# Linear attention and its tail: one elementwise step and one mask more taken off VectorE, the order changed, the expert layer begun inside the tail, and a weight test moved under the experts

## The reference, cut to what matters

```python
q = (elu(q) + 1.0) * scale
k = elu(k) + 1.0
attn = einsum('bhld,bhmd->bhlm', qi, ki) * causal
num = einsum('bhlm,bhme->bhle', attn, vi) + einsum('bhld,bhde->bhle', qi, S)
den = attn.sum(-1) + einsum('bhld,bhd->bhl', qi, Z)
out = num / maximum(den, 1e-06)
```

## Time and profile before

| | |
|---|---|
| median of 3 runs | 1272.51 us |
| the profiled execution: time, span | 1273.35 us, 1271.5 us |
| busy: TensorE, VectorE, ScalarE, GpSimd | 1152.8, 986.7, 771.9, 568.4 us |
| start to the first q and k | 0 to 26 us |
| linear attention, sequences 0 to 15 | 26 to 207 us |
| its tail | 207 to 237 us |
| experts | 237 to 436 us |
| softmax attention and FFN | from 437 us on |

### The profile page before, as it was taken

One profiled execution on the slowest core, in us unless ns is written; L12 is line 12 of the kernel. 1 busy time (PEld: TensorE's weight loads), 2 busy tenths in 40 slices (PEclk: granted clock), 3 DMA queues, 4 the chain that ended last, 5 costly groups with the idle time before them and its releaser, 6 DMA issues.

```text
span 1271.5 us, 32080 instructions
## 1 busy us (share of the span) xinstructions
PE 1152.8 (91%) x10554; PEld 941.7 (74%) x10554; DVE 986.7 (78%) x2499; ACT 771.9 (61%) x2314; POOL 568.4 (45%) x729
## 2 busy tenths in 40 slices
PE   3888886789898869999999999999999997999997
PEld 3555554688888747777777777777777766999997
DVE  6688885588888777778788778787877876788885
ACT  2445553222222249888989888899888894344342
POOL 2777775444444554444545445445444342011112
PEclk9999998799999989999999999999999998999999
DMA  8000000000000000000000000000000000000000
GB/s 282 10 2 0 0 1 2 1 2 1 0 1 0 1 1 2 1 2 1 2 2 1 0 0 0 0 0 0 0 0 0 2 1 1 6 13 12 8 12 19
DMA packets 14303, 12.32 MB, mean 10 GB/s; under 512 B 1778, under 2 KB 12564, under 8 KB 13972
## 3 DMA queue, kind: packets, MB, share of 16 engines
q1 hardware_dynamic: 14228, 11.34, 2.9%
HBM read 9.24 MB, written 2.10 MB: 9 GB/s over the span
## 4 chain that ended last, share of the span: by engine, by line
PE 56%; DVE 14%; issue 8%; POOL 4%; ACT 1%; DVEq 1%; POOLq 0%; ACTq 0%
PE bank L191 14%; PE bank L976 10%; PE bank L1041 10%; PE bank L1070 10%; PE bank L1083 5%; PE bank L840 4%; POOL rstd L365 2%; DVE stat L298 2%; DVE hT L1230 1%; DVE gg L1222 1%; PE bank L795 1%; DVE yn L314 1%; POOL X L370 1%; DVE mv L303 1%; DVE fh_hi L1191 1%
## 5 line engine op out<-in xcount | busy, mean ns | idle before, releaser
L993 ACT ACTIVATE work<-bank,work 128x256 f32<-128x256 f32 x512 | 236.0, 474 | 60.0 <-DVE work L985 59.2
L985 DVE TENSOR_REDUCE work<-bank 128x2 f32<-128x512 f32 x256 | 164.0, 682 | 113.2 <-PE bank L976 113.2
L1007 POOL TENSOR_TENSOR work<-work 128x512 f32<-128x512 f32 x64 | 66.7, 1041 | 279.0 <-DVE work L1001 279.0
L959 POOL TENSOR_TENSOR work<-work 128x512 f32<-128x512 f32 x128 | 164.3, 1284 | 30.2 <-DVE work L951 15.8
L1013 ACT ACTIVATE work<-work 128x256 f32<-128x256 f32 x384 | 161.7, 509 | 0.0
L1041 PE MATMUL bank<-ident,work 128*128 128x128 f32 x1024 | 141.9, 279 | 5.1 <-DVE work L949 1.6
L1041 PEld LDWEIGHTS bank<-ident,work 128*128 128x128 f32 x1024 | 111.7, 141 | 38.5 <-issue 19.9
L1070 PE MATMUL bank<-work 128*64 128x256 f32 x1024 | 138.5, 392 | 0.5 <-DVE work L1056 0.5
L840 PE MATMUL bank<-WrT,moe_work 128*128 128x128 f32 x1024 | 137.4, 278 | 0.7 <-POOL moe_work L817 0.7
L363 POOL TENSOR_SCALAR ve<-mv 128x2 f32<-128x2 f32 x128 | 28.6, 223 | 240.1 <-DVE mv L303 240.1
L976 PE MATMUL bank<-work 32*128 32x256 f32 x2048 | 130.4, 391 | 2.6 <-ACT work L993 1.6
(11 more groups left out here) (176 smaller groups left out, 2903.9 us busy)
## 6 DMA issues: line engine op xcount, KB each, us to landing
X<-in_x SPq DMA_DIRECT2D x4, 512.0 KB, 5.9
wF<-in_L_ffn_h_w SPq DMA_DIRECT2D x2, 1024.0 KB, 9.7
out<-X SPq DMA_DIRECT2D x16, 128.0 KB, 1.8
w_qkv<-in_L_attn_w_qkv SPq DMA_DIRECT2D x1, 1536.0 KB, 9.2
WrT<-in_L_ffn_Wr SPq DMA_DIRECT2D x1, 1024.0 KB, 5.1
w_out<-in_L_attn_w_out SPq DMA_DIRECT2D x1, 512.0 KB, 10.5
wF<-in_L_ffn_w_w SPq DMA_DIRECT2D x2, 256.0 KB, 8.5
rope_sin<-in_rope_sin SPq DMA_DIRECT2D x1, 256.0 KB, 3.2
```

Of the source, the lines that this page charges most:

```text
L959: nc.gpsimd.tensor_tensor((QT if kind == "q" else KT)[:, p, a, :], rc[:, ru % 2, :], rs_[:, ru % 2, :], ALU.add).then_inc(c_rope, 1)
L985: nc.vector.tensor_reduce(nmax[:, QUAD * a + j, :], SB_[j][:, :].rearrange("p (t k) -> p t k", t=T), AX.X, ALU.max, negate=True).then_inc( ...
L993: ins = nc.scalar.activation(pr[:, a % 2, j, t, :], SB_[j][:, t * LEN:(t + 1) * LEN], ACT.Exp, bias=nmax[:, h, t:t + 1], accum_out=psum_[: ...
```

## The change

1. The negative part goes to ScalarE: `Relu(-z)`, and the exponential reads it with scale -1. VectorE keeps one instruction for the feature.
2. Two of the four groups of masks per tile (`FAR_MASKS = 2`) go by ScalarE and GpSimd, and two stay on VectorE.
3. The order inside `la_step` changes on each engine. On TensorE v comes right after the scores of tile 0, and the turned norm, which uses v's place in PSUM, waits until v is copied (`a_va`); the output product follows it. On ScalarE the Relu and the exponential of the next sequence come first, and the copy of v goes ahead of that of the sums.
4. The experts' first copies of x are made in steps 14 and 15, Wsh in steps 2 and 3, and the first router product in step 15. The tail is written out: the norm of sequence 14 is interleaved with the first gates, spreads and scaled products, and the norm of sequence 15 moves into the first step of the experts. The order of the four spread banks changes, so that bank 2, still used by the norm, comes last.
5. The test of the ternary weights leaves the linear attention and stands at the end of each step of the experts, on GpSimd behind the far product of the next sequence's pair 3, on ScalarE one sequence later.

```diff
             last_use, per_seq = ((a_v, 1), (b_sh, 1))[l]
             pool.wait_ge(last_use, reached(per_seq * (i - 1)))
-            if l == MOE and i_is(i, 0, 1):
-                pool.wait_ge(a_v, SEQS)
+            if l == MOE:
+                if i_is(i, 0, 1):
+                    pool.wait_ge(a_v, SEQS - 1 + i)
                 pool.wait_ge(n_xnT[1], i + 1)
...
+        def la_feat_vector(dve, i, p):
+
+            dve.wait_ge(a_exp, i + 1)
+            dve.wait_ge(a_nd, reached(T * (i - 1)))
+            nc.vector.scalar_tensor_tensor(qk[:, p, :], QKB[:, :], 0.0, ex, ALU.max, ALU.add).then_inc(a_feat, 1)
+
+        def la_neg_scalar(act, i):
+
+            act.wait_ge(a_qk, i + 1)
+            act.wait_ge(a_exp, reached(i))
+            nc.scalar.activation(neg, QKB[:, :], ACT.Relu, scale=-1.0).then_inc(a_neg, 1)
...
-        RB, XB, YB_M = bank[1], bank[2:6], bank[6:8]
+        RB, XB, YB_M = bank[1], (bank[4], bank[5], bank[3], bank[2]), bank[6:8]
...
@@ GpSimd, la_step @@
-                la_mask_pool(pool, i, 0)
+                for g in range(FAR_MASKS):
+                    la_mask_pool(pool, i, 0, g)
...
-                if not i_is(i, SEQS - 2, SEQS - 1):
+                if i_is(i, SEQS - 2, SEQS - 1):
+                    pool_xT(pool, MOE, i - (SEQS - 2), p)
+                else:
                     pool_xT(pool, LA, i + 2, p)
...
                     norm_pool(pool, 1, i - LA_LAG, 1)
-                    ffn_excess_pool(pool, i - LA_LAG, p)
@@ GpSimd, after it @@
-            pool_xT(pool, MOE, 0, 0)
-            pool_xT(pool, MOE, 1, 1)
-            for i in range(SEQS - LA_LAG, SEQS):
-                for k in range(ROUNDS[1]):
-                    norm_pool(pool, 1, i, k)
-            for i in range(SEQS - LA_LAG, SEQS):
-                ffn_excess_pool(pool, i, i % 2)
-            pool.wait_ge(n_xnT[1], SEQS)
+            rstd_pool(pool, 1, SEQS - 2, 0)
+            residual_pool(pool, 1, SEQS - 2)
+            rstd_pool(pool, 1, SEQS - 2, 1)
 
             moe_far_pool(pool, 0, FAR)
 
             def moe_step(i, p):
-                lag = not i_is(i, 0)
-                if lag:
-                    rstd_pool(pool, 2, i - 1, 0)
+                r, of = (1, SEQS - 1) if i_is(i, 0) else (2, i - 1)
+                rstd_pool(pool, r, of, 0)
                 if not i_is(i, SEQS - 2, SEQS - 1):
                     pool_xT(pool, MOE, i + 2, p)
-                if lag:
-                    residual_pool(pool, 2, i - 1)
-                    rstd_pool(pool, 2, i - 1, 1)
+                residual_pool(pool, r, of)
+                rstd_pool(pool, r, of, 1)
                 moe_far_pool(pool, i, 4 + FAR)
-                if lag:
-                    rstd_pool(pool, 2, i - 1, 2)
+                if r == 2:
+                    rstd_pool(pool, r, of, 2)
                 if not i_is(i, SEQS - 1):
                     moe_far_pool(pool, i + 1, FAR)
+                ffn_excess_pool(pool, i, p)
@@ VectorE, la_step @@
+                if live:
+                    for g in range(FAR_MASKS, LA_GROUPS):
+                        la_mask_vector(dve, i, 0, g)
                 if not i_is(i, 0, 1, 2):
                     run_piece(1, n1, 3, i - LA_TURN_LAG, 1 - p)
-                if live:
-                    for g in range(1, LA_GROUPS):
-                        la_mask_vector(dve, i, 0, g)
+                if more:
+                    la_feat_vector(dve, i + 1, 1 - p)
                 if not i_is(i, 0, 1):
                     run_piece(1, n1, 0, i - LA_LAG, p)
...
@@ VectorE, the tail @@
+            la_state_vector(dve, SEQS - 1)
+            la_divide_vector(dve, SEQS - 1, 0)
+            run_piece(1, n1, 3, SEQS - 3, 1)
             for part in range(MOE_EXP_PART, MOE_ROUTER_PARTS):
                 moe_router_vector(dve, rch, 0, 0, part)
             rch.end()
+            run_piece(1, n1, 0, SEQS - 2, 0)
+            la_divide_vector(dve, SEQS - 1, 1)
+            run_piece(1, n1, 1, SEQS - 2, 0)
             moe_low_vector(dve, 0, 0)
+            moe_scaled_vector(dve, 0, 0)
+            moe_scaled_vector(dve, 0, 1)
+            run_piece(1, n1, 2, SEQS - 2, 0)
+            moe_scaled_vector(dve, 0, 2)
+            run_piece(1, n1, 3, SEQS - 2, 0)
...
@@ ScalarE, la_step @@
+                if more:
+                    la_neg_scalar(act, i + 1)
+                    la_exp_scalar(act, i + 1)
                 if live:
-                    la_mask_scalar(act, i, 0)
+                    for g in range(FAR_MASKS):
+                        la_mask_scalar(act, i, 0, g)
+                if more:
+                    la_v_scalar(act, i + 1, 1 - p)
                 if not i_is(i, 0):
                     la_sums_scalar(act, i - 1, 1)
                 if not i_is(i, 0, 1, 2):
                     norm_scalar(act, 1, i - LA_TURN_LAG, TB[:, 0:LEN])
                 if more:
-                    la_v_scalar(act, i + 1, 1 - p)
-                    la_exp_scalar(act, i + 1)
+                    la_blocks_scalar(act, i + 1, 1 - p)
...
@@ TensorE, la_step @@
                 if live:
                     la_scores_tensor(pe, i, p, 0)
-                if not i_is(i, 0, 1):
-                    la_out_tensor(pe, i - 2)
+                if more:
+                    la_v_tensor(pe, i + 1, 1 - p)
                 if not i_is(i, 0):
                     la_sums_tensor(pe, i - 1, 1 - p, 1)
                 if not i_is(i, 0, 1, 2):
+                    pe.wait_ge(a_va, at_most_all(i + 2))
                     pe.wait_ge(a_state, i)
                     norm_tensor(pe, 1, i - LA_TURN_LAG, TB)
-                if more:
-                    la_v_tensor(pe, i + 1, 1 - p)
+                if not i_is(i, 0, 1):
+                    la_out_tensor(pe, i - 2)
                 if not i_is(i, 0):
                     la_back_tensor(pe, i - 1, 1)
...
```

More of the change, by code:

```diff
@@ L1454, in _ @@
             dve.wait_ge(s_const, 16 * 7)
-            for part in range(2):
-                la_feat_vector(dve, 0, 0, part)
+            la_feat_vector(dve, 0, 0)
             n1 = norm_vector(dve, 1, chains[1], lambda p: Yt)
@@ L1476, in la_step @@
                     run_piece(1, n1, 1, i - LA_LAG, p)
-                if more:
-                    la_feat_vector(dve, i + 1, 1 - p, 1)
                 if live:
-                    for g in range(1, LA_GROUPS):
+                    for g in range(FAR_MASKS, LA_GROUPS):
                         la_mask_vector(dve, i, 1, g)
@@ L1483, in la_step @@
                     run_piece(1, n1, 2, i - LA_LAG, p)
+                if i_is(i, 2):
+                    dve.wait_ge(s_w[MOE], 16 * 4)
+                    nc.vector.tensor_tensor(Wsh[:, :], WsT[:, 0, :], WsT[:, 1, :], ALU.add).then_inc(s_wsh, 1)
+                if i_is(i, 3):
+                    dve.wait_ge(s_wsh, 1)
+                    dve.wait_ge(s_ident, 16)
+                    nc.vector.scalar_tensor_tensor(Wsh[:, :], Wsh[:, :], 0.5, ident[:, :], ALU.mult, ALU.add)\
+                        .then_inc(s_wsh, 1)
             over_sequences(dve, la_step, 4)
@@ L1514, in moe_step @@
                 for what, part in MOE_ORDER:
-                    if what == "norm" and not i_is(i, 0):
-                        run_piece(2, n2, part, i - 1, 1 - p)
+                    if what == "norm":
+                        if not i_is(i, 0):
+                            if i_is(i, 1) and part == len(n2) - 1:
+                                dve.wait_ge(n_tp[1], SEQS)
+                            run_piece(2, n2, part, i - 1, 1 - p)
+                        elif part in MOE_LAST_NORM:
+                            run_piece(1, n1, MOE_LAST_NORM.index(part), SEQS - 1, 1)
                     if what == "early" and not i_is(i, SEQS - 2, SEQS - 1):
@@ L1658, in _ @@
             moe_router_scalar(act, 1, 1)
-            for i in range(SEQS - 2, SEQS):
-                ffn_excess_scalar(act, i, i % 2)
             def moe_step(i, p):
@@ L1673, in moe_step @@
                     moe_far_scalar(act, i + 1, FAR)
+                if not i_is(i, 0):
+                    ffn_excess_scalar(act, i - 1, 1 - p)
             over_sequences(act, moe_step, 4)
@@ L1790, in _ @@
             pe.wait_ge(s_brlo, 1)
-            for k in range(4):
+            for k in range(FAR):
                 moe_spread_tensor(pe, 0, 0, k)
+            la_out_tensor(pe, SEQS - 1)
+            norm_tensor(pe, 1, SEQS - 2, TB)
+            pe.wait_ge(n_xnT[1], SEQS - 1)
+            moe_spread_tensor(pe, 0, 0, FAR)
             moe_router_tensor(pe, 1, 1)
@@ L1803, in moe_step @@
                         moe_spread_tensor(pe, i + 1, 1 - p, k - 4)
+                    if k == 0 and i_is(i, 1):
+                        norm_tensor(pe, 1, SEQS - 1)
                     if k == 0 and not i_is(i, 0, 1):
+                        if i_is(i, 2):
+                            pe.wait_ge(n_xnT[1], SEQS)
                         norm_tensor(pe, 2, i - 2)
```

100 lines of the change are left out of this document (39 added, 61 removed).

## The result

| | before | after |
|---|---|---|
| median of the runs, us | 1272.61 (1268.98 to 1273.03, 4 runs) | 1297.45 (1294.27 to 1300.47, 4 runs) |
| the profiled execution, us (its span) | 1273.35 (1271.5) | 1297.14 (1295.3) |
| mean granted clock of TensorE | 0.976 | 0.967 |

What follows compares the result with a forecast made beforehand. Steady linear attention was taken as a circle of TensorE, VectorE and ScalarE, the experts' as one over VectorE and GpSimd. First steps +1.6, steady -3.0, tail -12.7, experts +29.8 gave +15.7: 1288 us, range 1272 to 1302, own range 1280 to 1294.

Steps and rivals of the forecast that it cites:

- the rival with the lower clock: Experts: TensorE falls to the lower clock in each step, 13 x 0.9 = 12 us more, 1300; chance 0.14.
- Steady linear attention: Sequences 4 to 15: interval falls from 11.07 to 10.8 us, 11 x 0.27 = -3.0 us in all.
- 10.4 without the block: Steady linear attention: the interval would be 10.4 us if GpSimd's two masks did not hold up VectorE's xn.
- the wait for v's copy: Steady linear attention: the turned norm waits until ScalarE has copied v; TensorE goes on at 4.18 us, not 3.6.
- First steps: Early linear attention: waits for GpSimd's masks and for xn put score product 4 at 77.6 against 76.00, +1.6 us.
- Tail: From score product 15 to the experts' first shared product: 26.7 us against 39.4, so -12.7 us.
- Sign (2): Tail, in the changed profile: 25 to 28 us from score product 15 to the first shared product.
- the circle: Experts: a loop over VectorE and GpSimd, with the test's 2.72 us in it, makes the step 14.45 us against 12.52.
- The clock: Experts: a 3 us stop could lower TensorE's clock in each step; 0.9 us not hidden, step 15.3 us.
- Into and out of the experts: Around the experts' steps: +1.8 us before the first yn, +2.7 us where the attention waits behind sequence 15's test.
- that the test hides: Experts: the test fits under them, so 1.8, 24.4 and 0.9 us vanish and the time is 1261; chance 0.11.
- That the linear attention falls to 9.65: Linear attention: the step falls to TensorE's own 9.65 us, 12.6 us less, 1275.5; chance 0.15.

## Why the prediction was right, and where it was mis-sized

The sign and the mechanism were right; the sum was +15.7 us, measured were +23.8, at 1297 within the range and above the forecast's own (1280 to 1294). The 8.1 us between them are 1.0 in the first steps, 2.5 in the tail, 1.1 before the first yn of the experts, 3.6 and 1.5 in their steps and 0.7 behind these, less 2.2 in the rest of the kernel. That 1297 is near the 1300 of the rival with the lower clock is in good part chance, since the clock in the experts' steps is only a part of these.

- **Steady linear attention:** 10.8 forecast, 10.80 measured (-3.0 and -2.9 us). The stop before the turned norm is there, 1.35 us, with xn as its releaser; the second one is 0.16 us instead of 0.26. That the sum meets the measurement so closely is luck: the turned norm starts 5.04 us after the score product (137.51 - 132.47) and not 4.6, and the way from there to the next one is 5.8 us and not 6.2, two errors that cancel. The steps behind the number were tested one by one: "10.4 without the block" is 10.15 and 10.23 in two runs, the wait for v's copy is worth the 0.57 us that was forecast (0.55 measured, 10.23 to 9.68), and with both gone the step is TensorE's own (9.65 forecast).
- **First steps:** +1.6 forecast, +2.6 measured. Both waits that the prediction named are there, for GpSimd's masks at 59.35 and for xn at 71.35, 3.08 and 2.82 us long, and behind each the lower clock (the sums take 1.93 us, and the scores at 73.14 take 2.09 instead of 1.14). With one mask score product 4 comes 4.1 us earlier, with only GpSimd's second product gone 4.7, so this product weighs far more here than the 1.24 us that the prediction gave it: with one mask the first stop is 0.69 us, the second 2.28, and the clock behind the first stays full.
- **Tail:** -12.7 forecast, -10.2 measured. The turned norm was to come 16.0 us after score product 15 and came after 17.1 (214.51 - 197.37), the way from there to the first shared product took 12.0 us and not 10.7. From the product at 211.21 on the kernel ran at the lower clock (1.94 us for sums of 1.08; granted 0.63 up to the shared product), of which the prediction had only part. Sign (2) of the prediction asked for 25 to 28 us and got 29.2. With one mask the turned norm comes after 14.8 us, its sums at the full clock, and the whole stretch is 26.2 us. Of the 10.2 us, 1.9 come with the test alone: with it out of the old tail the stretch is 37.5 instead of 39.4.
- **Experts:** the circle was worked to 14.45 us and 14.4 taken; a step at the full clock is 14.44. The terms are as worked too: 1.89 us from the negated maximum to the far product, 1.05 to the first product, 2.78 for the three, 1.05 from there to yn. The mis-sized step is "**The clock**": it was not put into the sum. In 7 of the 14 steps the clock was below 1.00. The first 13 steps took 28.0 us more than before, not 24.4; at 14.45 us each they would have taken 24.2 more, so some 3.8 fall to the lower clock. Half of that lies in one step of 16.39 us, where the lower clock came behind the stop of 2.46 us and the pairs took 2.06 us for eight products. The last step took 2.4 us more, not 0.9, and as much with the test moved alone (13.96 against 11.60). The rival that has the lower clock in each step was half right in how often, and mostly wrong in the price: at 0.88 and 0.89 the steps were 14.5 to 15.0 us (the last one 14.0). The Trainium skill, "TensorE: Matmul & The Clock Gate", in "HAM oscillation — how this bites in real kernels", describes loops that pay in every round; this loop did in some.
- **Into and out of the experts:** before the first yn +2.9 instead of +1.8. From shared product to yn it is 19.58 us here, 18.00 with the test in the attention (one product is still in this stretch), 17.59 without the test: its share is 1.6 to 2.0, and the other 0.9 to 1.3 come with the rest of the change. At the end the test's share is 17.78 - 15.08 = 2.70 us, as forecast; 0.65 lie on the other edits. What follows the last yn, put at nothing, was 2.2 us shorter than before; in the kernels that leave the softmax attention and the FFN as they are it is 825.2 to 828.0 us long (825.8 here, 828.0 before), and what makes this spread stays open.
- **The rivals:** that the test hides was excluded at three products (1.06 us of slack hold one). That the linear attention falls to 9.65 needs two edits that the change doesn't have.

By medians: the test in the experts +32.2 (1297.45 - 1265.27), the new linear attention and tail -6.8 (1265.27 - 1272.08), the test out of the old ones -1.3. With one mask of four and the output product ahead of the turned norm the new order is worth 31.7 us (1272.08 - 1240.36). Taken in this order, the mask gives 15.0 of it and the output product 9.9; the other way round they give 5.4 and 19.5, so the two are not independent.

## What to carry to other kernels

Before work is moved into an engine's idle time, look at two things: what is queued behind it there (slack of 1.06 us takes one product of 0.7, not three), and what VectorE, which shares ports with GpSimd, does in that moment. Work for GpSimd goes where VectorE reads PSUM or where another engine sets the pace: under the attention, with TensorE busy 498 of the 500 us from 500 to 1000 in that kernel, 45 products were nearly free. An operation that must wait should stand behind the one that needn't.

## What the runs showed of the hardware

- GpSimd's products and some of VectorE's operations exclude each other in whole instructions. xn is two instructions of 0.33 us each, 0.59 us as a pair; beside GpSimd's two mask products of 1.25 us each the pair took 2.33 us. The small operation with two inputs in SBUF (128x64) took 0.85 us instead of 0.23 beside a product; masks and scaled products that read PSUM kept their 0.64 and 0.69 us. The Trainium skill, "SBUF — State Buffer", "Who interferes with whom", has this rule, and the rows agree. New is how much hangs on it: 1.7 us for one pair in a step of 10.8.
- The lower clock came in some steps and not in others of the same loop, with nearly the same stop: 1.00 in the step from 363.11 (2.66 us), 0.79 in that from 406.95 (2.46 us). It is not mere scatter, since in the kernel before with only the test moved the twelfth step is again the long one, 16.40 us at 0.79. What tells the steps apart stays open.
